# First edge layer computed in the expert phase, three result buffers, and a later turn in the edge loop

## The reference, cut to what matters

```python
x = x + L0_gnn(xn, ...) + L0_mix(xn, ...)
x = x + L0_ffn(layernorm(x), ...)                       # six experts, three layers each, relu
xn = layernorm(x)
x = x + L1_gnn(xn, ..., edge_attr_4, edge_attr_8, ...) + L1_mix(xn, ...)
x = x + L1_ffn(layernorm(x), ...)
# L1_gnn, h0 and h1 are linear in the node features:
hid = silu(edge_attr_8 @ fc_w0 / sqrt(8))               # E x 64, the first edge layer
w = hid @ fc_w1 / sqrt(64)                              # E x 256
xs0, xs1 = h0[edge_src], h1[edge_src]
mid = products of w, xs0, xs1 and edge_attr_4           # E x 512
y = segment_sum(mid, edge_dst)                          # N x 512
```

## Time and profile before

| | us |
|---|---|
| runs | 3961.5, 3962.7, 3972.2 |
| median | 3962.7 |
| profiled execution, its span | 3966.1 |
| expert phase (2167 to 2506) | 339 |
| norm and galerkin (2506 to 2652) | 146 |
| edge loop (2652 to 3356) | 704 |
| the rest behind it | 610 |

### The profile page before, as it was taken

How to read it: one execution, slowest core, us unless ns; L and a number is a source line. 1 busy time by engine, 2 the same in 40 slices (tenths; PEclk the granted TensorE clock), 3 DMA queues, 4 the chain that set the end, 5 groups by cost and what they waited for, 6 DMA issues and landing times. The chain is left out here.

```text
span 3966.1 us, 60201 instructions
## 1 busy us (share of the span) xinstructions
PE 3642.8 (92%) x18935; PEld 3087.8 (78%) x18935; DVE 2451.9 (62%) x4843; ACT 1491.9 (38%) x3475; POOL 665.9 (17%) x658
## 2 busy tenths in 40 slices
PE   5999899999999999999996999988888888869996
PEld 2555699999999998999994888657777777848885
DVE  7886655555555555556554666556666665677775
ACT  0363311211211111112114544457777775136663
POOL 0002000000000000000002200025555553012221
PEclk9999999999999999999997999989999999879998
DMA  1353022222222222222222210112222222431113
GB/s 53 65 105 65 26 87 89 65 89 84 70 84 74 80 88 71 83 83 71 83 69 98 72 31 30 42 47 83 81 84 79 84 80 59 150 71 38 38 38 119
DMA packets 265216, 288.48 MB, mean 73 GB/s; under 512 B 70331, under 2 KB 237327, under 8 KB 264283
## 3 DMA queue, kind: packets, MB, share of 16 engines
q1 hardware_dynamic: 233701, 208.44, 18.1%
q0 software_dynamic: 24192, 66.15, 5.8%
q10 hardware_dynamic: 7030, 10.16, 0.7%
HBM read 242.21 MB, written 42.48 MB: 72 GB/s over the span
## 5 line engine op out<-in xcount | busy, mean ns | idle before, releaser
L1043 PE MATMUL bank<-a_wide,parts 125*128 125x448 f32 x4200 | 872.9, 367 | 0.0
L1043 PEld LDWEIGHTS bank<-a_wide,parts 125*128 125x128 f32 x4200 | 785.6, 188 | 78.4 <-issue 9.9
L2288 POOL DMA_INDIRECT rows<-h_dram,src_t x392 | 375.4, 958 | 331.9 <-DVE prod L2483 218.7
L2421 ACT ACTIVATE hot<-eq,ea 128x80 f32<-128x80 f32 x1568 | 405.3, 352 | 1.0 <-DVE eq L2463 0.5
L1093 DVE CAST a_wide<-a_cols 125x2240 fp32r<-125x2240 bf16 x210 | 275.5, 1328 | 138.7 <-PE bank L1043 138.7
L1017 POOL TENSOR_TENSOR nf_g<-nf,nf_g 128x896 fp32r<-128x896 f32 x42 | 95.4, 2271 | 1575.0 <-ACT nf_g L1187 1575.0
L2328 PEld LDWEIGHTS bank<-prod,hot 128*80 128x80 f32 x2352 | 295.9, 153 | 70.9 <-issue 21.6
L2328 PE MATMUL bank<-prod,hot 128*80 128x128 f32 x2352 | 331.8, 277 | 10.6 <-issue 10.4
L1052 PE MATMUL bank<-nf_g,whh 128*128 128x448 f32 x1512 | 339.7, 369 | 0.0
L1052 PE MATMUL bank<-msg,wc 128*128 128x448 f32 x1512 | 339.1, 369 | 0.0
L1052 PEld LDWEIGHTS bank<-msg,wc 128*128 128x128 f32 x1512 | 284.2, 188 | 27.5
(11 more groups left out here) (438 smaller groups left out, 5787.7 us busy)
## 6 DMA issues: line engine op xcount, KB each, us to landing
a_cols<-a_dram SPq DMA_DIRECT2D x210, 546.9 KB
a_dram<-a_cols SPq DMA_DIRECT2D x15, 1250.0 KB, 9.9
w<-in_w SPq DMA_DIRECT2D x4, 2728.0 KB
deg_bc<-deg_dram SPq DMA_DIRECT2D x42, 224.0 KB, 6.0
gate_bc<-gate_dram SPq DMA_DIRECT2D x42, 224.0 KB, 3.2
rows<-h_dram,src_t POOLq DMA_INDIRECT x392
w<-y_rows SPq DMA_DIRECT2D x12, 512.0 KB, 15.1
w<-in_w SPq DMA_DIRECT2D x6, 896.0 KB
```

The lines of the kernel that those rows point to most:

```text
L1043: ins = nc.tensor.matmul(p_msg[f][:, 0:GW], parts[0:SPB, m, c * HB + k, f * 128:(f + 1) * 128], a_wide[u % 2][0:SPB, k, :], start=(c == 0 ...
L2288: nc.gpsimd.indirect_dma_start(out=rows[n % ITC][:, :], out_offset=None, in_=h_dram, in_offset=bass.IndirectOffsetOnAxis(ap=src_t[:, n:n + ...
L2421: ins = nc.scalar.activation(hot[:, q % 2, j, m, :], eq[:, q % 2, j, :], ACT.Copy, scale=ea4[:, q * UC + j, m:m + 1])
```

## The change

Three things are done.

The first edge layer moves into the expert phase. There, 98 pieces of HE = 256 columns are computed; a column holds two edges, one of each of two neighbouring units, packed above each other on the 128 partitions, with `fw` a block matrix of 128x128. Piece n = 3(i - 5) + spot runs in step i = 5 to 37: spot 0 behind `layer1`, spot 1 behind `layer2`, spot 2 behind `layer3` and the turn. Per piece PE makes one matmul into `bank[7]`, ACT two silus of 128x256 out of it (one rounded to fp32r, one not), POOL the low part, and SP issues three loads of 16 rows for piece n + 3 and one store of 256 KB to `hid_dram`. There are three buffers for results (`hid`) and three for attributes (`ea`). The turn of a tile moves from the start of a step to behind `layer3`, into the one bank `p_x[0]` for all but the last tiles, and it waits for the addition of the tile before.

In the edge loop `hidden`, `silu`, `split` and the load of `ea8` are gone. SP loads each unit's `hid` with two transfers of 128 KB, up to HIDS = 7 units ahead, and `weights(q, 0)` waits for them.

`turn(q-1)` moves from behind chunk 1 of unit q to the end of unit q. DVE's `add` becomes that of q - 2 and stands between products 0 and 1.

Besides, the loads, memsets and splits of `fw0` and `ea8` go from `norm_and_galerkin` and `ea8_dram` has 16 rows instead of 24; `adjacency` has one more register instruction per tile on ACT (the count is kept from falling below zero).

```diff
-                        act.reg_add(turns, turns, rounds)
+                        act.reg_alu(more, rounds, 0, ALU.max)
+                        act.reg_add(turns, turns, more)
...
-                for at_row, part, ready in ((0, 0, ea_high), (16, 0, ea_high), (8, 1, ea_low)):
+                for at_row, part, ready in ((0, 0, ea_high), (8, 1, ea_low)):
...
+        ea = [sb(ctx, f"ea{b}", [128, HE], F32R) for b in range(3)]
+        fw_raw = sb(ctx, "fw_raw", [128, 128])
+        fw_high = sb(ctx, "fw_high", [128, 128], F32R)
+        fw = sb(ctx, "fw", [128, 128], F32R)
+        hid = sb(ctx, "hid", [128, 3, PARTS, HE], F32R)
...
-        p_h1, p_h2, p_y, p_x = bank[0:2], bank[2:4], bank[4:6], bank[6:8]
+        p_h1, p_h2, p_y, p_x, p_hid = bank[0:2], bank[2:4], bank[4:6], bank[6:8], bank[7]
+
+        def piece(i, spot):
+
+            n = 3 * (i - FIRST_STEP) + spot
+            return range(n, n + 1) if 0 <= n < PIECES else range(0)
+
+        def turned_in(t):
+            return p_x[0] if t < SOON else p_x[t % 2]
...
+                def edges(n):
+                    if n < PIECES:
+                        i, h = divmod(n, 2)
+                        units = ea8_dram.rearrange("(m a) (i u c) -> m i u a c", m=PARTS, i=NIT, u=2)[:, i, :, :, h * HE:(h + 1) * HE]
+                        sp.dma_start(ea[n % 3][0:16, :].bitcast(F32), units[0]).then_inc(ea_in[n % 3], 16)
+                        sp.dma_start(ea[n % 3][16:32, :].bitcast(F32), units[1]).then_inc(ea_in[n % 3], 16)
+                        sp.dma_start(ea[n % 3][32:48, :].bitcast(F32), units[0]).then_inc(ea_in[n % 3], 16)
+
+                def move(n):
+                    i, h = divmod(n, 2)
+                    sp.wait_ge(hid_mm, START + n + 1)
+                    edges(n + 3)
+                    sp.wait_ge(hid_low, START + n + 1)
+                    sp.dma_start(hid_dram[i, :, :, h * HE:(h + 1) * HE].rearrange("m p e -> p m e"), hid[:, n % 3, :, :].bitcast(F32))\
+                      .then_inc(hid_out[n % 3], 16)
...
+                sp.dma_start(fw_raw[:, :], A["fw0"]).then_inc(fw_in, 16)
+                sp.wait_ge(ea_zero, START + 3)
+                for n in range(3):
+                    edges(n)
...
-                for i in range(4, NI):
-                    gate_load(i)
+                for i in range(4, NI + 4):
+                    for n in piece(i - 4, 0):
+                        move(n)
+                    if i < NI:
+                        gate_load(i)
+                    for spot in (1, 2):
+                        for n in piece(i - 4, spot):
+                            move(n)
                     if i == WKV_AT:
...
             def _(pool):
+                for b in range(3):
+                    nc.gpsimd.memset(ea[b][:, :].bitcast(F32), 0.0).then_inc(ea_zero, 1)
...
+                pool.wait_ge(fw_in, START + 16)
+                nc.gpsimd.tensor_copy(fw_high[:, :], fw_raw[:, :]).then_inc(fw_step, 1)
+                pool.wait_ge(fw_step, START + 1)
+                nc.gpsimd.tensor_tensor(fw[:, :], fw_raw[:, :], fw_high[:, :], ALU.subtract).then_inc(fw_step, 1)
+                pool.wait_ge(fw_step, START + 2)
+                nc.gpsimd.tensor_copy(fw[0:32, :], fw_raw[0:32, :]).then_inc(fw_step, 1)
+                for n in range(PIECES):
+                    pool.wait_ge(silu_done, START + n + 1)
+                    nc.gpsimd.tensor_tensor(hid[:, n % 3, 1, :], hid[:, n % 3, 1, :].bitcast(F32), hid[:, n % 3, 0, :], ALU.subtract)\
+                      .then_inc(hid_low, 1)
...
+                def edge_layer(n):
+                    pe.wait_ge(fw_step, START + 3)
+                    pe.wait_ge(gate_done, START + 1)
+                    pe.wait_ge(ea_in[n % 3], START + n // 3 * 48 + 48)
+                    pe.wait_ge(silu_done, START + n)
+                    nc.tensor.matmul(p_hid[:, 0:HE], fw[:, :], ea[n % 3][:, :], start=True, stop=True).then_inc(hid_mm, 1)
+
                 def turn(t):
-                    pe.wait_ge(added, START + t - 1)
+                    if t < SOON:
+                        pe.wait_ge(added, START + t)
+                    else:
+                        pe.wait_ge(added, START + t - 1)
+                        pe.wait_ge(silu_done, START + PIECES)
                     for k in range(KD):
-                        ins = nc.tensor.transpose(p_x[t % 2][0:RT, k * 128:(k + 1) * 128], xt[:, k, t * RT:(t + 1) * RT], ident[:, :])
+                        ins = nc.tensor.transpose(turned_in(t)[0:RT, k * 128:(k + 1) * 128], xt[:, k, t * RT:(t + 1) * RT], ident[:, :])
                     ins.then_inc(turned, 1)
                 layer1(0)
                 for i in range(NI + 2):
+                    if i + 1 < NI:
+                        layer1(i + 1)
+                    for n in piece(i, 0):
+                        edge_layer(n)
+                    if i < NI:
+                        layer2(i)
+                    for n in piece(i, 1):
+                        edge_layer(n)
+                    if 0 < i <= NI:
+                        layer3(i - 1)
                     for t in turns(i):
                         pe.wait_ge(y_out, START + (i - 1) // E0 * KD)
                         turn(t)
-                    if i + 1 < NI:
-                        layer1(i + 1)
-                    if i < NI:
-                        layer2(i)
-                    if 0 < i <= NI:
-                        layer3(i - 1)
+                    for n in piece(i, 2):
+                        edge_layer(n)
...
+                def edge_layer(n):
+                    act.wait_ge(gate_out, START + 64)
+                    act.wait_ge(b3_low, START + 2)
+                    act.wait_ge(hid_mm, START + n + 1)
+                    act.wait_ge(hid_out[n % 3], START + n // 3 * 16)
+                    for m in range(PARTS):
+                        to = hid[:, n % 3, m, :]
+                        ins = nc.scalar.activation(to if m == 0 else to.bitcast(F32), p_hid[:, 0:HE], ACT.Silu,
+                                                   scale=8.0 ** -0.5)
+                    ins.then_inc(silu_done, 1)
...
             def _(sp):
-                per_round = (NU, DMAS)
+                per_round = (NCH,)
                 rounds, regs = begin(sp, "sp", per_round)
                 with sp.Fori(0, rounds) as r:
-                    units, dmas = at_round(sp, regs, per_round)
+                    chunks, = at_round(sp, regs, per_round)
                     for q in range(NU):
-                        b = q % 2
-                        sp.wait_ge(hid_mm, units + q - 1)
-                        sp.dma_start(ea8[0:24, b, :].bitcast(F32), ea8_dram[:, q * UE:(q + 1) * UE]).then_inc(ea_in[b], 16)
+                        pair, u = divmod(q, 2)
+                        sp.wait_ge(w_mm, chunks + max(q - HIDS + 1, 0) * UC)
+                        for m in range(PARTS):
+                            sp.dma_start(hid[m * MUL:(m + 1) * MUL, q % HIDS, :].bitcast(F32),
+                                         hid_dram[pair, m, u * MUL:(u + 1) * MUL, :]).then_inc(hid_in[q % HIDS], 16)
                     next_round(sp, regs, per_round)
...
                     def weights(q, j):
                         if j == 0:
-                            pe.wait_ge(hid_done, units + q + 1)
+                            pe.wait_ge(hid_in[q % HIDS], loads + q // HIDS * 32 + 32)
                         pe.wait_ge(p_done, chunks + q * UC + j + 1 - UC)
                         for m in range(PARTS):
...
-                    hidden(0)
                     for j in range(UC):
                         weights(0, j)
-                    hidden(1)
                     for q in range(NU):
-                        if q + 2 < NU:
-                            hidden(q + 2)
                         for j in range(UC):
                             sums(q, j)
                             if q + 1 < NU:
                                 weights(q + 1, j)
-                            if j == 1 and q:
-                                turn(q - 1)
+                        if q:
+                            turn(q - 1)
                     turn(NU - 1)
                     next_round(pe, regs, per_round)
...
-                    silu(0)
                     weighted_hots(0)
-                    silu(1)
                     for q in range(NU):
                         if q:
                             copy(q - 1)
-                        if q + 2 < NU:
-                            silu(q + 2)
                         if q + 1 < NU:
                             weighted_hots(q + 1)
                     copy(NU - 1)
...
                     one_hots(0)
-                    split(0)
                     one_hots(1)
-                    split(1)
                     for j in range(UC):
                         products(0, j)
                     for q in range(NU):
                         if q + 1 < NU:
                             products(q + 1, 0)
+                        if q > 1:
```

(43 more changed lines are left out.)

81 lines of the change are left out of this document (35 added, 46 removed).

## The result

| | before | changed |
|---|---|---|
| runs | 20 | 20 |
| median, us | 3967.5 | 3978.3 |
| lowest and highest | 3960.4, 3974.9 | 3970.1, 3985.9 |
| profiled execution, its span | 3966.1 | 3973.8 |

What follows compares the result with a forecast made beforehand. PE was taken to bound the expert phase, and pauses between trains of gathers the edge loop. Loop -24 and expert phase +12 gave -12 us off the median 3962.7: 3951 us, range 3870 to 3992.

Steps and rivals of the forecast that it cites:

- The expert phase, +12: Expert phase: 98 added PE pieces at 0.20 us cost 19.6 us, the turn's wait saves 7.9; from +5 to +35.
- The loop, -24: Edge loop: fewer trains (runs of successive gathers), split waits and an earlier start save 24 us, from 0 to -45.
- PE can issue one more chunk ahead of the turn, and the next train has one more gather: Edge loop: moving the turn lengthens trains of gathers from 4.61 to 4.99, 6.4 fewer trains, -16 us.
- 2.45 us for each pause: Edge loop: time modelled as 392 gathers at 1.25 us plus 85 trains, each adding 2.45 us.
- The split, 0 to -17.6, taken at -6: Edge loop: PE's 25 waits for L2459, 17.6 us in all, go; worth 0 to -17.6 us, taken at -6.
- the start: Edge loop's start: hot, silu and a table load no longer precede the first weights; 0 to -4 us, taken at -2.
- The pauses as a part of the kernel: Edge loop: POOL's gathers come in 85 trains with pauses, PE's work being seen some 1.9 us late.
- The gathers set the unit: Edge loop: buffers, not the turn, end trains, so the loop gains nothing; 3975 us, up to 3998; chance 0.25.
- PE as the bound of the loop: Edge loop: pauses weaken, the loop falls towards PE's own 549 us; halfway, 3897 us for the kernel; chance 0.17.
- The bottom of the loop's range, -45: Edge loop: best case, each train one whole gather longer, worth 37 us, and the split.

Runs made afterwards that it cites:

- The turn alone: Kernel before with only the turn moved to the unit's end, the addition to q - 2, and one register instruction: ratio 0.9974 on the first chip, 1.0011 on the third.
- the memset of 0.17 us: Changed kernel with a POOL memset of 128x64 behind each gather of the edge loop: 3980.8 us in one run on the first chip.

## Why the prediction was wrong

The range, 3870 to 3992, held the 3978; the sign was wrong.

- *The expert phase, +12.* Near, +14.4, but in part by luck. Two errors of 7 and 8 us cancel: a piece costs PE 0.12 us and not 0.20, and the loads' place on SP ahead of the weights, and the long step beside `wkv` with the lower clock behind it, cost 8 us that the sum had at nothing. The prediction named SP's order only for the stores, and had SP's issues at half their cost.
- *The loop, -24.* Wrong on this chip, -3. The step that failed is "PE can issue one more chunk ahead of the turn, and the next train has one more gather", at -16 us. The first half came true (waits at the turn 47.6 to 13.3 us), the second didn't: a train has 4.2 gathers in the mean and not 4.99, and the pauses are 92 and not 79. A train is ended by the eight buffers, and they are kept by products that start late because PE's finished weights are counted late. This the change left as it was: 82 late products and 217 us before, 92 and 311 after. The reading of the earlier trace rows took the delay for 1.9 us behind the newest weights; it is 4.3 behind those that the product needs.
- *2.45 us for each pause.* This was a fit to one trace, not a mechanism. The turn alone has 25 pauses more than before and a loop 9 us shorter; the memset of 0.17 us takes 13 pauses from the changed kernel and nothing from its loop.
- *The turn's worth.* Alone it gives 9 us in the loop, and with the first layer gone nothing. Why is open.
- *The split, 0 to -17.6, taken at -6, and the start.* Not separable on this chip. On the third chip the loop gains 5 us beyond PE's 22.5. That is not the split's wait there, for PE waits for it once, 3.3 us, at the start.
- *The pauses as a part of the kernel.* This is the assumption under all of it, and it fell: on two other chips PE's counts in the loop are on time, and the same program is 3% faster. Why PE's counts come late on the first chip is open.
- *The gathers set the unit*, the third rival, gave the right time, 3975. A part of its reason is in the trace: the buffers end the trains. But rows in flight have no share in it (a gather waits for a product), and the gathers do not set the pace: late products do. With the same eight buffers and PE's work counted on time the loop is 125 us shorter.
- *PE as the bound of the loop*, the second rival, is what the third chip shows: 98 x 5.60 = 549 from its working, 539 measured from first to last gather.
- *The bottom of the loop's range, -45,* does not add up as written: 37 and the split's 17.6 are 55.

## What to carry to other kernels

Where several engines see one engine's finished work in the same late moment, ask first whether that is the kernel's doing. Here the semaphores' times in the trace said whose counts are late, and a second chip said that the kernel is not enough to make them so. Work taken from an engine pays where that engine sets the pace; here it paid 28 us on the third chip, 22.5 of them PE's own, and 3 on the one where PE's work was counted late, against 14 to 16 us for the place it moved to. A cost per event that is fitted to one trace is not a mechanism: count the events again in a variant. For work moved into another phase, cost every DMA issue by its own shape, and look at what it stands ahead of on its queue.

## What the runs showed of the hardware

The same program took 3968 us on one chip and 3844 and 3845 on two others, with nearly equal clocks (0.967 and 0.971) and equal durations of the instructions. The difference lies in the edge loop, 692 and 567 us. On the slower one PE's counts of finished work in that loop came late and in bursts, 4.3 us in the pause shown, while DVE's and ACT's were on time, and elsewhere PE's were too. There a gap of 0.41 us between indirect gathers took 35 us off the loop and one of 0.17 took nothing; on the second and third chip the gap of 0.41 made the kernel before 1.0% slower. A load of 16 rows of 1 KB holds SP for 0.60 us, the broadcast gate load for 0.35. POOL's subtraction of 128x256 beside DVE's cast of 128x896 lengthened the cast from 0.63 to 1.05 us, and mostly left DVE's two-input multiplication at 1.09.
